# Attention edges rewritten (rows normalised on ScalarE, wide cross product, ones rows), and two node-stage stores begun by ScalarE's queue

## The reference

```python
x = _layernorm(x + _L0_gnn_ref(x, node_vec1, edge_attr_4, edge_attr_8, ..., src, dst), axis=-1)
x = _layernorm(x + _L1_gnn_ref(...), axis=-1)
x = _layernorm(x + _L2_gnn_ref(...), axis=-1)
x = _layernorm(x + _L3_gnn_ref(x, node_vec1, edge_attr_3, edge_attr_64, src, dst, ...), axis=-1)
# the edge part of the fourth layer
s, v = _eq_ln(node_input, ln1_w0, ln1_b0, ln1_w1)
ms = (s @ msrc_ws)[edge_src] + (s @ mdst_ws + mdst_bs)[edge_dst]      # mv: the same for vectors
h = jax.nn.silu(_ln(edge_scalars @ rw1 + rb1, rg1, rbe1))
h = jax.nn.silu(_ln(h @ rw2 + rb2, rg2, rbe2))
w1, w2, w3, w4, w5 = jnp.split(h @ rw3 + roff, ...)
ds = concat([w1 * ms, w4 * (mv . Y1) / SQ3])                          # Y1: the edge's direction
dv = concat([(w2 * ms)[:, :, None] * Y1[:, None, :], w3 * mv, w5 * cross(mv, Y1) / SQ2])
ls, lv = _eq_lin(ds, dv, lin_ws, lin_bs, lin_wv)                      # logits, values
a = einsum('ehk,hk->eh', _smooth_leaky(alpha), alpha_dot)             # then a softmax per destination
```

## Time and profile before

| What | Value |
|---|---|
| median of 3 runs | 11330.98 us (11328.65 to 11331.06) |
| profiled execution | 11326.82 us, span 11325.1 us |
| mean granted TensorE clock | 0.88 of full speed |
| busy share of the span | PE 80%, PEld 73%, DVE 72%, ACT 40%, POOL 47% |
| DMA | 753.89 MB, mean 67 GB/s |
| transfers of SP's queue / of POOL's | 18.4% / 6.0% of 16 engines' span |

### The profile page before, as it was taken

The page is one execution under the profiler, slowest core; times in us unless marked ns, Lnnn a source line. Parts: engine busy times, 40 slices in busy tenths (PEclk is TensorE's granted clock), DMA queues, the critical chain, the costliest instruction groups (busy, mean ns, idle before and its releaser), DMA issues. The chain is left out here.

```text
span 11325.1 us, 241587 instructions
## 1 busy us (share of the span) xinstructions
PE 9089.1 (80%) x58771; PEld 8291.2 (73%) x58771; DVE 8098.2 (72%) x40535; ACT 4475.4 (40%) x17107; POOL 5279.8 (47%) x6680
## 2 busy tenths in 40 slices
PE   7877787777778787799978887888588888849998
PEld 6777777777777777688866676777577777738888
DVE  5666666666666666688878887888688888877777
ACT  4555555555555555333322232333222222212222
POOL 3444444444444444577755554555444444423444
PEclk8888888888888888899999998999888888869999
DMA  2222222222222222233322222222111111111111
GB/s 68 85 86 85 85 86 85 86 86 85 86 86 85 86 85 85 70 77 77 77 63 68 68 67 59 57 57 57 39 40 40 39 39 40 39 32 51 53 54 48
DMA packets 988491, 753.89 MB, mean 67 GB/s; under 512 B 430970, under 2 KB 948478, under 8 KB 988048
## 3 DMA queue, kind: packets, MB, share of 16 engines
q1 hardware_dynamic: 823696, 587.78, 18.4%
q0 software_dynamic: 164352, 162.20, 6.0%
HBM read 362.41 MB, written 392.80 MB: 67 GB/s over the span
## 5 line engine op out<-in xcount | busy, mean ns | idle before, releaser
L749 ACT ACTIVATE nodes_x<-nodes_z 125x161 f32<-125x161 f32 x2400 | 1005.5, 422 | 1439.1 <-DVE nodes_z L673 1437.4
L127 PE MATMUL bank<-ident 128*128 128x128 f32 x10000 | 1478.0, 297 | 97.1 <-PEq L883 58.7
L127 PEld LDWEIGHTS bank<-ident 128*128 128x128 f32 x10000 | 1415.1, 213 | 145.5 <-issue 59.2
L814 PE MATMUL bank<-self_v,nodes_v_t 128*125 128x98 f32 x4800 | 1153.2, 328 | 0.0
L812 PE MATMUL bank<-self_s,nodes_s_t 128*125 128x65 f32 x4800 | 977.2, 291 | 150.9 <-DVE ffn_y L233 143.6
L812 PEld LDWEIGHTS bank<-self_s,nodes_s_t 128*125 128x125 f32 x4800 | 879.8, 223 | 226.6 <-issue 206.4
L612 POOL TENSOR_SCALAR nodes_z<-nodes_sum 125x2 f32<-125x2 f32 x400 | 113.2, 283 | 1987.4 <-DVE nodes_sum L663 1987.4
L673 DVE SCALAR_TENSOR_TENSOR nodes_z<-bank,nodes_z 125x162 f32<-125x162 f32 x2400 | 811.2, 380 | 273.7 <-PE bank L814 271.4
L1203 POOL DMA_INDIRECT table<-edge_new,edge_into_now x600 | 733.5, 1222 | 565.5 <-issue 516.4
L312 PE MATMUL bank<-ident,ffn_sn 125*65 125x125 f32 x800 | 264.6, 346 | 788.3 <-DVE ffn_sn L214 784.3
L663 DVE TENSOR_REDUCE nodes_sum<-nodes_z 125x2 f32<-125x322 f32 x400 | 195.4, 489 | 948.8 <-DMA nodes_z<-rows 948.8
(11 more groups left out here) (496 smaller groups left out, 30563.3 us busy)
## 6 DMA issues: line engine op xcount, KB each, us to landing
table<-nodes_z SPq DMA_DIRECT2D x1200, 160.2 KB
nodes_z<-rows SPq DMA_DIRECT2D x400, 160.2 KB
out<-nodes_res SPq DMA_DIRECT2D x400, 156.2 KB
nodes_v_t<-x_t SPq DMA_DIRECT2D x400, 94.7 KB
edge_dst_row<-dst SPq DMA_DIRECT2D x300, 122.1 KB
ordered<-edge_new SPq DMA_DIRECT2D x200, 160.2 KB
edge_rows<-ordered SPq DMA_DIRECT2D x200, 160.2 KB
dest_rows<-kept SPq DMA_DIRECT2D x100, 316.4 KB
```

The lines of the kernel that those rows point to most:

```text
L127: pe.matmul(banks[2 * ((n + lead) % LANES) + odd][:, 0:128], w["ident"][:, :], w["ident"][:, :], start=True, stop=True)
L749: ins = act.activation(x3[:, k, :], z[:, l + 1, k, 0:X], ACT.Square, bias=z[:, l + 1, k, MEAN:MEAN + 1], scale=-1.0, accum_out=total[:, l, ...
L814: ins = pe.matmul(banks[2 + n % 2][0:P, o + MEAN:o + A + 1], xv[:, n, c], w[f"self_v{l}"][:, :], start=False, stop=True, skip_group_check= ...
```

## The change

In `all_nodes`, the store of the third table (`store3`) and the store of the output (`store_out`) are issued by ACT's queue in place of SP's, with the same waits and addresses; their due times are 37.98 and 71.77 in place of 35.98 and 71.47.

In `attention_edges`:
- `divide` and `normalize` leave DVE. DVE only forms offsets, minus mean times root (`offsets`, five small instructions, two of which scale the edge's direction), and ACT normalises the rows with scale and bias (ten instructions), the kept destination row among them.
- The biases of the radial layers and of the `outputs` matmul are rows of the weights, which meet a row of ones in the turned operands (row 64 of `attr_t` and `h`, row 96 of `p4`). `h_add` and `bias` are gone, and what read their results reads PSUM.
- Silu takes the place of Identity, Tanh and the DVE step `h_gate`.
- The cross product: the `outputs` matmul writes five columns for each vector (x y z x y), so that three products of 192 columns (`cross0`), one difference, one sum and one sum with PSUM replace the 18 instructions. `leak` is one instruction, and its factor 0.4 is in `alpha_dot`.
- The 16 filling matmuls become six, behind `linear`. ACT copies the gather's index (`keep_attr`).
- A new `order` with `part` 13.00.

The set-up of the weights follows (copies in place of halvings, bias rows, memsets). SP's `load` waits for `offsets`, its `store` for the copied values too, and `turn_attr` on PE for `leak`, `cross3` and the copied values of the round before.

```diff
-             ("store3", 35.98), ("root3", 36.68), ("offset3", 37.63), ("divide", 37.9), ("shift", 39.2),
+             ("store3", 37.98), ("root3", 36.68), ("offset3", 37.63), ("divide", 37.9), ("shift", 39.2),
...
-            def store_out(n, i):
-                sp.wait_ge(t["act"][n], count_at(t, i + 1, "act", "out_normed"))
-                gate(sp, t)
-                sp.dma_start(out_view[:, bass.ds(i * T + J * n, J), :], res[:, tiles(n), :]
-                             ).then_inc(out_stored[n], 16)
-
-            run_rounds(sp, rounds, order, part, dict(load=load_x, store_out=store_out, store1=store_table(1),
-                                                     store2=store_table(2), store3=store_table(3)), lanes)
...
+            def store3(n, i):
+                act.wait_ge(t["dve"][n], count_at(t, i + 1, "dve", "widened2"))
+                gate(act, t)
+                act.dma_start(table_view[3][:, bass.ds(i * T + J * n, J), :], z[:, 3, tiles(n), :]
+                              ).then_inc(stored[3][n], 16)
+
+            def store_out(n, i):
+                act.wait_ge(t["act"][n], count_at(t, i + 1, "act", "out_normed"))
+                gate(act, t)
+                act.dma_start(out_view[:, bass.ds(i * T + J * n, J), :], res[:, tiles(n), :]
+                              ).then_inc(out_stored[n], 16)
+
...
+    part = 13.00
+    order = [("load", 0.0), ("measure", 5.54), ("merge", 7.7), ("turn_attr", 9.71), ("copy_attr", 10.22),
+             ("differences", 10.3), ("hidden1", 10.63), ("squares", 10.87), ("h_measure1", 11.21),
+             ("add_squares", 11.46), ("widen", 11.68), ("roots", 11.9), ("offsets", 13.74), ("normalize", 14.31),
+             ("h_merge1", 14.36), ("h_widen1", 14.66), ("h_roots1", 14.9), ("h_normalize1", 15.66),
+             ("turn_h1", 16.16), ("activate1", 16.76), ("turn_src", 16.96), ("hidden2", 17.31),
+             ("copy_src", 17.61), ("h_measure2", 17.89), ("h_merge2", 18.3), ("h_widen2", 19.67),
+             ("h_roots2", 19.9), ("keep_attr", 20.08), ("gather_next", 20.52), ("turn_dst", 20.77),
+             ("copy_dst", 21.42), ("h_normalize2", 21.48), ("turn_h2", 22.04), ("activate2", 22.55),
+             ("turn_vec", 23.07), ("copy_vec", 23.58), ("spread_vec", 23.99), ("copy_spread", 24.6),
+             ("linear", 25.01), ("copy_linear", 26.54), ("weights", 27.23), ("products", 29.01),
+             ("product4", 30.38), ("outputs", 30.8), ("cross0", 32.75), ("cross1", 33.53), ("copy_values", 33.7),
+             ("take_tanh", 34.07), ("cross2", 34.3), ("cross3", 34.83), ("leak", 35.19), ("dot", 35.52),
+             ("add_heads", 35.84), ("store", 36.18)]
+
...
-    part = 17.05
-    order = [("load", 0.0), ("turn_attr", 2.7), ("measure", 2.7), ("copy_attr", 3.3), ("merge", 4.25),
...
-    fill = [(3, 1, 3), (1, 0, 2), (0, 0, 5), (0, 0, 3), (0, 0, 3)]
...
             def gather_next(n, i):
 
-                p.wait_ge(gathered[n], 64 * i + 64)
-                gate(p, t)
-                p.wait_ge(t["dve"][n], count_at(t, i + 1, "dve", "normed"))
+                p.wait_ge(t["act"][n], count_at(t, i + 1, "act", "normed"))
                 gate(p, t)
                 p.wait_ge(t["act"][n], count_at(t, i + 1, "act", "attr_kept"))
                 gate(p, t)
-                gather(n, i + 1)
+                gather(n)
...
-            def divide(n, i):
+            def offsets(n, i):
 
                 v.wait_ge(t["pool"][n], count_at(t, i + 1, "pool", "roots"))
-                v.wait_ge(kept_stored[n], 48 * i + 48)
-                for j in range(J):
...
+                y = e["y"][:, J * n:J * n + J, :]
+                scale = root[:, n, 10:12].unsqueeze(2)
+                v.tensor_tensor(r[:, n, :, 0:3], y[:, :, 0:3], scale.broadcast_to([P, J, 3]), ALU.mult)
+                v.tensor_tensor(r[:, n, :, 3:5], y[:, :, 0:2], scale.broadcast_to([P, J, 2]), ALU.mult)
+                v.scalar_tensor_tensor(offset[:, n, 0:4].unsqueeze(2), mom[:, n, 0, :, 0:1], -1.0,
+                                       root[:, n, 0:4].unsqueeze(2), ALU.mult, ALU.mult)
+                v.scalar_tensor_tensor(offset[:, n, 4:8].unsqueeze(2), rows_of(n)[:, :, MEAN:MEAN + 1], -1.0,
+                                       root[:, n, 4:8].unsqueeze(2), ALU.mult, ALU.mult)
+                one(v.scalar_tensor_tensor(offset[:, n, 8:10].unsqueeze(2), e["rows"][:, n, 1, :, MEAN:MEAN + 1], -1.0,
+                                           root[:, n, 8:10].unsqueeze(2), ALU.mult, ALU.mult), n)
...
-                def h_add(n, i):
+                def hidden_of(n, j):
+                    return banks[2 * n + 1][0:P, 256 + j * 64:320 + j * 64]
+
+                def h_measure(n, i):
...
-            def bias(n, i):
+                one(v.tensor_tensor(p4[0:V, n, :], p4[0:V, n, :], spread[:, n, :], ALU.mult), n)
+
+            def three(n):
+                return [terms[:, n, k, :, :, :] for k in range(3)]
+
+            def wide_of(n, first):
+                x = vectors_of(n)[:, :, U:6 * U].rearrange("p j (w c) -> p j w c", c=5)[:, :, :, first:first + 3]
+                return x
+
+            def turned_r(n, first):
+                return r[:, n, :, first:first + 3].unsqueeze(2).broadcast_to([P, J, U, 3])
+
+            def cross0(n, i):
                 v.wait_ge(t["pe"][n], count_at(t, i + 1, "pe", "outputs"))
-                for j in range(J):
-                    k, bank = J * n + j, banks[2 * n + j]
...
+                along, plus, minus = three(n)
+                v.tensor_tensor(along, vectors_of(n)[:, :, 0:U].unsqueeze(3).broadcast_to([P, J, U, 3]),
+                                turned_r(n, 0), ALU.mult)
+                v.tensor_tensor(plus, wide_of(n, 1), turned_r(n, 2), ALU.mult)
+                one(v.tensor_tensor(minus, wide_of(n, 2), turned_r(n, 1), ALU.mult), n)
+
+            def cross1(n, i):
+                after(i, n, "cross0")
+                along, plus, minus = three(n)
+                one(v.tensor_tensor(plus, plus, minus, ALU.subtract), n)
+
+            def cross2(n, i):
+                after(i, n, "cross1")
+                along, plus, minus = three(n)
+                one(v.tensor_tensor(plus, plus, along, ALU.add), n)
+
+            def cross3(n, i):
+                after(i, n, "cross2")
+                v.wait_ge(t["act"][n], count_at(t, i + 1, "act", "tanh"))
+                gate(v, t)
+                v.wait_ge(kept_stored[n], 48 * i + 48)
+                gate(v, t)
+                one(v.tensor_tensor(keep[:, J * n:J * n + J, S:F],
+                                    heads_of(n)[:, :, 128:224],
+                                    three(n)[1].rearrange("p j w c -> p j (w c)"), ALU.add), n)
...
-                one(v.tensor_scalar(tanh[:, n, :, :], tanh[:, n, :, :], 0.4, 0.6, ALU.mult, ALU.add), n)
-
-            def leaked(n, i):
-                after(i, n, "leak")
-                one(v.tensor_tensor(alpha[:, n, :, :], alpha[:, n, :, :], tanh[:, n, :, :], ALU.mult), n)
+                one(v.scalar_tensor_tensor(alpha[:, n, :, :], tanh[:, n, :, :], 1.5, heads_of(n)[:, :, 0:64],
+                                           ALU.add, ALU.mult), n)
...
-                    x = banks[2 * n + 1][0:64, 0:W]
-                    act.activation(h_u[:, n, :], x, ACT.Identity, bias=w["rbe"][:, k:k + 1],
-                                   scale=w["rg"][:, k:k + 1])
-                    one(act.activation(h_tanh[:, n, :], x, ACT.Tanh, bias=w["rbe"][:, 2 + k:3 + k],
-                                       scale=w["rg"][:, 2 + k:3 + k]), n)
+                    one(act.activation(e[("h", "h2")[k]][0:64, n, :], banks[2 * n + 1][0:64, 0:W], ACT.Silu,
+                                       bias=w["rbe"][:, k:k + 1], scale=w["rg"][:, k:k + 1]), n)
                 return step
+
+            def normalize(n, i):
+
+                wait("dve", n, i, "offsets")
+                act.wait_ge(kept_stored[n], 48 * i + 48)
+                for j in range(J):
+                    for side, x in enumerate((e["xs"], e["xd"])):
+                        k, row = side * J + j, e["rows"][:, n, side, j, :]
+                        act.activation(x[:, n, j, 0:S], row[:, 0:S], ACT.Identity, bias=offset[:, n, k:k + 1],
+                                       scale=root[:, n, k:k + 1])
+                        act.activation(x[:, n, j, S:F], row[:, VS:X], ACT.Identity, bias=offset[:, n, 4 + k:5 + k],
+                                       scale=root[:, n, 4 + k:5 + k])
+                    ins = act.activation(keep[:, J * n + j, X3:X3 + X], e["rows"][:, n, 1, j, 0:X], ACT.Identity,
+                                         bias=offset[:, n, 8 + j:9 + j], scale=root[:, n, 8 + j:9 + j])
+                one(ins, n)
 
...
             def keep_attr(n, i):
-                wait("dve", n, i, "x3")
-                one(act.activation(keep[:, J * n:J * n + J, ATTR + 1:ATTR + 2], e["rows"][:, n, 1, :, A:A + 1],
-                                   ACT.Copy), n)
```

(35 more changed lines are left out.)

188 lines of the change are left out of this document (71 added, 117 removed), and 8 rows, old and new, of the table order.

## The result

The changed kernel is slower by 0.8%: median 11,423.41 us (11,418.72 to 11,428.21, three runs) against 11,330.98; ratio 1.0082, 95% interval 1.0059 to 1.0105. I had forecast 11,076 with a range to 11,240. Its profiled execution has a span of 11,416.6 us, 91.5 more than before.

A forecast was written before the change was run, and what follows sets the result against it. Node stage bound by one full DMA engine (gain 0), attention edges by POOL's gather loop: 243 us from steps of 16.4 in place of 18.83, plus 12 for the shorter pipeline, took 11,331.0 to 11,076 us; range 10,800 to 11,240.

The forecast's parts named there:

- what bounds it: Node stage: one DMA engine with too many packets sets the step, which stays 11.49 us.
- SP itself was the bound: Node-stage rival: SP's issuing sets the step, so 9.3 us a step, -880 us, 10,196; chance 0.08.
- ACT would be held as SP is: Node-stage rival: ACT's two stores wait behind the full queue, 13.9 us a step, +950, 12,025; chance 0.06.
- the stores' worth: Node stage: moving two stores from SP to ACT gains 0; each 0.1 us a step would be worth 40 us.
- Work on each engine: Attention edges, per step: DVE 10.0 us, ACT at most 10.8, PE 12.2 at the same clock.
- POOL's loop of 15.8 us: Attention edges: POOL's gathers and roots (9.2 us) and DVE's part (6.6) are walked once a step and bound it.
- a second loop: Attention edges: from `offsets` through ACT, PE and `products` to POOL's part again, about 32 us over two steps, 16 a step.
- The clock: Attention edges: TensorE's granted clock stays 0.84, which slows the 32 us loop by some 0.5 us.
- my 16.4: Attention edges: step time taken, 16.4 us in place of 18.83, between 15.2 and 18; gain 243 us.
- "The clock" (18 us a step, 11,250): Attention-edge rival: with ten fills less TensorE falls to 1.2 GHz for most of the stage, gain 80 us; chance 0.14.
- the vector engine was the bound: Attention-edge rival: DVE's fall from 15.8 to 10 us gives steps of 13.5 to 14, -500 us, 10,830; chance 0.17.
- The 12 us for the pipeline's end: Attention edges: the last lane's way through the shorter pipeline is shorter, some 12 us gained once.

The follow-up runs named there:

- single split load: Changed kernel with the node stage's second `x_t` load (97 partitions) issued as two, 96 partitions and 1: 10,314.23 us, ratio 0.9108.
- stores-only run: Kernel before with only the two node-stage stores moved to ACT's queue: 11,263.90 us, ratio 0.9942.
- run with the fills: Changed kernel, its six filling matmuls behind `linear` kept, with eleven more in PE's waits: 11,136.32 us, ratio 0.9834.
- early `h_normalize2`: Changed kernel with `h_normalize2` due at 19.70 in place of 21.48, ahead of `cross0`, `cross1`, `merge` and `cross2` on DVE: 11,129.79 us, ratio 0.9827.

## Why the prediction was wrong

- **Node stage, what bounds it: right.** A full DMA engine (inferred, as said above); a single split load gave 1,109 us. That SP itself was the bound and that ACT would be held as SP is, both fell: ACT's store takes 0.27 us in the stores-only run's trace, and one more issue on SP was no hindrance. (The table rows of one partition are 2 x 164 floats, 1,312 bytes, and not the 1,304 given ahead of the prediction; no sum uses it.)
- **Node stage, the stores' worth: a term mis-sized.** I took 0 and measured 66 us (0.16 us a step), within the "each 0.1 us a step is worth 40 us" that I kept open. Why two queues let the full engine get on faster was not settled.
- **Work on each engine: right.** DVE 777.29 / 78 = 10.0 us a step (forecast 10.0), ACT 647.80 / 78 = 8.3 (at most 10.8), `normalize` 3.7 (3.4), products of 192 columns 0.35 (0.35).
- **The loop: the first of two steps that failed.** I wrote that POOL's loop of 15.8 us "must be walked once a step" and is the bound, and that a second loop takes "about 32 us at full TensorE clock, 16 a step". Doubling the roots changed nothing, though POOL's part came out as forecast (9.3 us from `h_roots2` at 9015.35 to `offsets` at 9024.62, forecast 9.2) and so did both of its signs: `roots` right behind the last gather, DVE waiting 2.53 us for it. The second loop was drawn too long: its part from `h_normalize2` over `turn_h2`, `linear`, fills, `weights`, `products` and `outputs` back to the cross steps closes in a single step. At a clock of 0.94 it takes 17.6 us, 1.2 more than my 16.4. In the row of due times, `h_normalize2` at 21.48 (8.48 modulo 13.00) stands behind `cross0` at 6.75: that could be read off the change.
- **The clock: the second step that failed.** "With ten fills less and a shorter step PE's share stays about the same, so I keep 0.84" and "+0.5 us". It fell to 0.75, and 287 us came back with fills. PE's busy share did stay (77% of the stretch, 81% before); what it did not tell is where PE rests, 2.5 us in one piece, and that just the part in the loop ran slow. Counted by the run with the fills, 2.8 of the 4.0 us between 16.4 and 20.4 went with the clock and 1.2 with the loop. Counted by the early `h_normalize2`, 2.8 went with one due time, 1.7 of it the rest alone. The two overlap, so no run divides the 4.0 us cleanly between the two failed steps.
- **Rivals.** "The clock" (18 us a step, 11,250) came nearest and was still 2.4 us a step short, because it had the clock without the loop. That the vector engine was the bound fell: it went from 84% to 49% busy (I had forecast 60%) and the step grew.
- **POOL's loop exists, one size longer.** It was the bound once the other was shortened: 17.2 us, not 15.8, since it goes through ACT's `normalize`, `turn_src` and `hidden2` (4.9 us), which I had left out in favour of `products`.
- **The 12 us for the pipeline's end** did not show: from the last `att_root` to the end of the span it is 11325.1 - 10016.3 = 1308.8 us before and 11416.6 - 10107.6 = 1309.0 after.

## What to carry to other kernels

Write down every loop through the new order, each engine's neighbours included, before an order is trusted: one due time, which put a short instruction behind work that waits for the loop's own result, was worth 294 us here. A wait that the trace shows is not yet a bound: DVE waited 2.53 us a step for `roots`, and making `roots` twice as long cost nothing. Filling matmuls are part of a schedule; whoever takes work out of the other engines and the fills with it should look at the longest rest of PE and at the clock of the stretch behind it, not at its mean busy share. And when an issue takes microseconds, count how many DMA engines a transfer really uses before moving it to another queue.

## What the hardware showed

- The same 250-column matmul took 0.58 or 1.04 us, by the granted clock. In the changed kernel, with rests of 2.49 and 2.58 us, the rate was down 1.5 and 1.1 us after work began again. With rests of 1.24 us it fell too where waits of 0.3 to 0.6 us followed, and did not where fills stood in these. Rests of 1.42 and 1.47 us passed without a fall with fills around them (clock 0.94 and 0.96), and 1.84 and 1.47 us close together did not (0.80). So the longest rest alone doesn't tell it.
- Removing six matmuls (2.6 us a step at 1.2 GHz) from the middle of the binding loop changed the time by nothing measurable; adding eleven made the kernel 287 us faster; with the order changed, five of them made the step 1.1 us longer.
- A load of 97 rows of 1,000 bytes, issued as 96 and 1, took 1,109 us off 11,423.
- Moving two stores to ACT's queue was worth -66 us with one DMA engine full, and +28 us (0.08 us a step) with it relieved.
